# A four-stage graph network: narrow one-hots per 50 columns, and wide one-hots of two and three tiles in turn

## The reference

```
h = max(layernorm(x), 0);  x = x + L0(h)   # 4 rounds of y = segment_sum(weight * y[dst], src)
h = max(layernorm(x), 0);  x = x + L1(h)   # second stage, one round
h = max(layernorm(x), 0);  x = x + L2(h)   # two rounds by relation type, log_softmax
h = max(layernorm(x), 0);  x = x + L3(h)   # last stage, one round
```

```
# second stage: bx, by are 4 hat functions each of the edge's two attributes
msg = sum over u, v of bx[u] * by[v] * (h[dst] @ W[u, v])          # [edges, 16]
out = segment_sum(msg, src, 12500)
# last stage: 8 attributes per edge
m   = silu(einsum('ei,ej,ijh->eh', h[dst], edge_attr_8, W) / sqrt(128))
out = segment_sum(m @ W_lin / 4, src, 12500)
```

## Time and profile before

| | |
|---|---|
| time before | 18148.49 us, median of 3 (18147.04 to 18175.33) |
| profiled execution | span 18161.1 us from its first to its last instruction, 349,411 instructions; it gives no other time of its own |
| busy over the span | PE 15098.9 us (83%), DVE 14620.2 (81%), ACT 11849.6 (65%), POOL 10508.1 (58%) |
| second stage, `conv` | first `product` at 8874.0 us, last at 10899.5 us, 330 of them |
| last stage, `message` | first `product` at 15873.0 us, last at 17955.2 us, 330 of them |
| granted TensorE clock | 1.00 in both stages' loops, 0.897 on average over the span |

### The profile page before, as it was taken

The page is one execution under the profiler, slowest core; times in us unless marked ns, Lnnn a source line. Parts: engine busy times, 40 slices in busy tenths (PEclk is TensorE's granted clock), DMA queues, the critical chain, the costliest instruction groups (busy, mean ns, idle before and its releaser), DMA issues. The chain is left out here.

```text
span 18161.1 us, 349411 instructions
## 1 busy us (share of the span) xinstructions
PE 15098.9 (83%) x83251; PEld 13315.7 (73%) x83252; DVE 14620.2 (81%) x36172; ACT 11849.6 (65%) x23181; POOL 10508.1 (58%) x29948
## 2 busy tenths in 40 slices
PE   0148847998998999899699998999969999499997
PEld 0048846887887888789688885777747777399996
DVE  4745557887887888788699997999958888499997
ACT  2000026777777777678577777888858888377775
POOL 0458836775775775777477765666622424376610
PEclk9555558999999999999899999999989999699998
DMA  7611121010000100000211112222211212111111
GB/s 233 125 26 40 40 78 27 23 24 22 23 24 22 24 24 23 23 24 24 34 31 31 31 25 65 73 71 72 74 43 61 67 61 67 33 31 31 30 27 17
DMA packets 1268447, 826.81 MB, mean 46 GB/s; under 512 B 873458, under 2 KB 1213398, under 8 KB 1260758
## 3 DMA queue, kind: packets, MB, share of 16 engines
q1 hardware_dynamic: 880918, 671.78, 13.2%
q0 software_dynamic: 269056, 117.80, 3.5%
q10 hardware_dynamic: 118080, 33.61, 1.0%
HBM read 587.33 MB, written 235.06 MB: 45 GB/s over the span
## 5 line engine op out<-in xcount | busy, mean ns | idle before, releaser
L1548 PE MATMUL powers_sums<-powers_b_hot,powers_spread 128*128 128x224 f32 x26400 | 5284.7, 361 | 670.8 <-DVE powers_b_hot L1529 455.7
L1548 PEld LDWEIGHTS powers_sums<-powers_b_hot,powers_spread 128*128 128x128 f32 x26400 | 5097.4, 195 | 860.3 <-issue 826.7
L1650 POOL DMA_INDIRECT filled<-powers_by_b,powers_at_start x2688 | 3364.3, 1252 | 1721.6 <-issue 847.3
L2351 PE MATMUL relate_got<-relate_hot,relate_table 112*128 112x512 f32 (+1 forms) x10560 | 3091.5, 435 | 110.8 <-ACT relate_hot L2313 70.5
L1543 ACT ACTIVATE powers_b_hot<-powers_away,ones 128x672 f32<-128x672 f32 x2640 | 1977.9, 751 | 1251.6 <-PE powers_sums L1548 880.1
L1537 ACT ACTIVATE powers_away<-wide,powers_minus_b 128x224 f32<-128x224 f32 x6600 | 2717.6, 472 | 117.5 <-ACT powers_minus_b L1718 35.0
L2351 PEld LDWEIGHTS relate_got<-relate_hot,relate_table 112*128 112x128 f32 x10560 | 1702.7, 191 | 1388.5 <-issue 1315.0
L1526 DVE TENSOR_TENSOR powers_spread<-powers_a_hot,powers_message 128x640 f32<-128x640 f32 x2640 | 2154.4, 816 | 517.5 <-PE powers_sums L1548 327.8
L2313 ACT ACTIVATE relate_hot<-relate_away,ones 112x1280 f32<-112x1280 bf16 x1320 | 1797.9, 1362 | 734.3 <-PE relate_got L2351 447.3
L1529 DVE TENSOR_SCALAR powers_b_hot<-wide,powers_b_val 128x224 f32<-128x224 f32 x6600 | 1918.5, 339 | 0.0
L2366 PE MATMUL relate_mixed<-relate_mix,relate_picked 128*128 128x128 f32 x13200 | 1711.4, 277 | 107.3 <-issue 92.2
(11 more groups left out here) (475 smaller groups left out, 25622.2 us busy)
## 6 DMA issues: line engine op xcount, KB each, us to landing
relate_codes<-pair_rows SPq DMA_DIRECT2D x264, 800.0 KB
powers_given<-filled SPq DMA_DIRECT2D x528, 200.0 KB
rec<-relate_running SPq DMA_DIRECT2D x132, 400.0 KB
filled<-powers_by_b,powers_at_start POOLq DMA_INDIRECT x2688
grouped<-order_blanks POOLq DMA_DIRECT2D x20, 1320.0 KB
filled<-order_blanks SPq DMA_DIRECT2D x20, 1320.0 KB
held_recs<-grouped SPq DMA_DIRECT2D x132, 200.0 KB
conv_given<-filled SPq DMA_DIRECT2D x132, 200.0 KB
```

The source lines that it names most:

```text
L1548: mm = pe.matmul(gathering.sums[:, bass.ds(group * STRIDE, WINDOW)], spread[:, j].rearrange("p a d -> p (a d)"), b_hot[:, j, :], start=Fal ...
L1650: pool.indirect_dma_start(filled, bass.IndirectOffsetOnAxis(to, 0), rows, None).then_inc(spread_out[block % 2], 16)
L2351: mm = pe.matmul(got[:, n % 2, at:to], table[:, n // SLOTS % 2, half, :], flat[:, at:to], start=half == 0, stop=half == 1, skip_group_chec ...
```

## The change

`a_hot`, `b_val` and ScalarE's `minus_b` are made once for a pair (50 columns, two halves of an iteration as buffers) instead of once for a unit (10 columns). `own` becomes a pair of numbers, one for each slot of a unit: (2, 3) in the second stage, (2, 2) in the last. In the second stage the slot with 3 tiles makes them with one `tensor_tensor` compare of 3 x 224 instead of three `tensor_scalar` compares, and ScalarE makes 3 tiles of the first slot and 2 of the second.

```diff
@@ -1519,12 +1519,16 @@
     return dram.rearrange("(h p) d -> p h d", p=P)
 
 
-def spread_slot(dve, message, a_hot, spread, b_val, b_hot, c, ready, own):
+def spread_slot(dve, message, a_hot, spread, b_val, b_hot, c, ready, own, at_once=False):
 
 
     n = message.shape[1]
     dve.tensor_tensor(spread, a_hot.unsqueeze(3).to_broadcast([P, n, 8, D]),
                       message.unsqueeze(2).to_broadcast([P, n, 8, D]), ALU.mult)
+    if at_once:
+        dve.tensor_tensor(b_hot[:, 0:own, :], b_val[:, 0:own].unsqueeze(2).to_broadcast([P, own, WINDOW]),
+                          c.wide[:].unsqueeze(1).to_broadcast([P, own, WINDOW]), ALU.is_equal).then_inc(ready, 1)
+        return
     for j in range(own):
         ins = dve.tensor_scalar(b_hot[:, j, :], c.wide[:], b_val[:, j:j + 1], None, ALU.is_equal)
     ins.then_inc(ready, 1)
@@ -1780,8 +1784,8 @@
         fourth = half if hats else s.sb("fourth", [P, UNIT, 2, D])
         message = s.sb("message", [P, 2, UNIT, D])
         active = s.sb("active", [P, 2, UNIT, D]) if silu_scale is not None else message
-        a_hot = s.sb("a_hot", [P, 2, UNIT, 8])
-        b_val = s.sb("b_val", [P, 2, UNIT])
+        a_hot = s.sb("a_hot", [P, PAIRS_PER, PAIR * TURN, 8])
+        b_val = s.sb("b_val", [P, PAIRS_PER, PAIR * TURN])
         spread = s.sb("spread", [P, SPREADS, TILES, 8, D])
         b_hot = s.sb("b_hot", [P, SPREADS, TILES, WINDOW])
         if hats:
@@ -1794,9 +1798,9 @@
             turns_of, rows_of, across = 2, TILES * D, P
         mix = s.sb("mix", [rows_of, 1 if hats else TILES, P])
         turned = s.sb("turned", [rows_of, 2, turns_of, P])
-        own = 3 if hats else 2
-        away = s.sb("away", [P, 2, TILES - own, WINDOW])
-        minus_b = s.sb("minus_b", [P, 2, UNIT])
+        own = OWN if hats else (2, 2)
+        away = s.sb("away", [P, 2, TILES - min(own), WINDOW])
+        minus_b = s.sb("minus_b", [P, PAIRS_PER, PAIR * TURN])
         measured, warmed, copied_b, gate_act, gate_pe = (
             s.sem(n) for n in ("measured", "warmed", "copied_b", "gate_act", "gate_pe"))
         still, rested = s.sb("still", [P, RESTS]), s.sem("rested")
@@ -1943,20 +1947,24 @@
             def warm(it, first, j):
 
                 u = it * UNITS + j
-                act.copy(minus_b[:, j % 2], G.minus_b[:, bass.ds(u * UNIT, UNIT)]).then_inc(copied_b, 1)
-                act.wait_ge(copied_b, u + 1)
+                h, at = j // PER_PAIR, j % PER_PAIR * UNIT
+                if at == 0:
+                    pair = it * PAIRS_PER + h
+                    act.copy(minus_b[:, h], G.minus_b[:, bass.ds(pair * (PAIR * TURN), PAIR * TURN)]).then_inc(copied_b, 1)
+                    act.wait_ge(copied_b, pair + 1)
                 for part in range(2):
                     if not (first and j == 0):
                         act.sem_inc(gate_act, 1)
                         act.wait_ge(warmed, 2 * u + part - 1)
-                    away_from(act, c, minus_b[:, j % 2, part * TILES + own:(part + 1) * TILES], away[:, part], measured)
+                    away_from(act, c, minus_b[:, h, at + part * TILES + own[part]:at + (part + 1) * TILES],
+                              away[:, part, 0:TILES - own[part]], measured)
                 for part in range(2):
                     slot = 2 * j + part
                     act.wait_ge(measured, 2 * u + part + 1)
                     if not first or slot >= SPREADS:
                         act.sem_inc(gate_act, 1)
                         act.wait_ge(taken, 2 * u + part - SPREADS + 1)
-                    warm_slot(act, c, away[:, part], b_hot[:, slot % SPREADS, own:TILES], warmed)
+                    warm_slot(act, c, away[:, part, 0:TILES - own[part]], b_hot[:, slot % SPREADS, own[part]:TILES], warmed)
 
             if hats:
                 act.wait_ge(set_up, 1)
@@ -2026,17 +2034,20 @@
                                   along[:, j // PER_PAIR, at:at + UNIT].unsqueeze(2).to_broadcast([P, UNIT, 4, D]),
                                   ALU.mult).then_inc(zed, 1)
 
-            def scatter(u, j, first):
-
-                dve.wait_ge(mid, u + 1)
+            def scatter(it, j, first):
+
+                u = it * UNITS + j
+                h, at = j // PER_PAIR, j % PER_PAIR * UNIT
+                dve.wait_ge(mid, it * PAIRS_PER + h + 1)
                 dve.wait_ge(summed if silu_scale is None else activated, u + 1)
                 for part in range(2):
                     slot = 2 * j + part
                     if not first or slot >= SPREADS:
                         dve.wait_ge(taken, 2 * u + part - SPREADS + 1)
                     tiles = slice(part * TILES, (part + 1) * TILES)
-                    spread_slot(dve, active[:, j % 2, tiles], a_hot[:, j % 2, tiles], spread[:, slot % SPREADS],
-                                b_val[:, j % 2, tiles], b_hot[:, slot % SPREADS], c, ready, own)
+                    cols = slice(at + part * TILES, at + (part + 1) * TILES)
+                    spread_slot(dve, active[:, j % 2, tiles], a_hot[:, h, cols], spread[:, slot % SPREADS],
+                                b_val[:, h, cols], b_hot[:, slot % SPREADS], c, ready, own[part], at_once=own[part] == 3)
 
             scans(0, 0, 0, D)
             if hats:
@@ -2064,11 +2075,11 @@
                                       co.unsqueeze(3).to_broadcast([P, UNIT, v_wide, D]), ALU.mult).then_inc(times, 1)
                     if not first or j >= 2:
                         dve.wait_ge(ready, 2 * (u - 1))
-                    dve.tensor_tensor(a_hot[:, j % 2], G.a[:, bass.ds(u * UNIT, UNIT)].unsqueeze(2)
-                                      .to_broadcast([P, UNIT, 8]),
-                                      c.free[:, 0:8].unsqueeze(1).to_broadcast([P, UNIT, 8]), ALU.is_equal)
-                    dve.tensor_scalar(b_val[:, j % 2], G.minus_b[:, bass.ds(u * UNIT, UNIT)], -1.0, None, ALU.mult
-                                      ).then_inc(mid, 1)
+                    if jj == 0:
+                        cols = bass.ds((it * PAIRS_PER + h) * (PAIR * TURN), PAIR * TURN)
+                        dve.tensor_tensor(a_hot[:, h], G.a[:, cols].unsqueeze(2).to_broadcast([P, PAIR * TURN, 8]),
+                                          c.free[:, 0:8].unsqueeze(1).to_broadcast([P, PAIR * TURN, 8]), ALU.is_equal)
+                        dve.tensor_scalar(b_val[:, h], G.minus_b[:, cols], -1.0, None, ALU.mult).then_inc(mid, 1)
                     dve.wait_ge(times, u + 1)
                     dve.tensor_tensor(half[:], product[:, :, 0:v_wide // 2, :], product[:, :, v_wide // 2:v_wide, :],
                                       ALU.add).then_inc(added, 1)
@@ -2080,10 +2091,10 @@
                     dve.tensor_tensor(message[:, j % 2], fourth[:, :, 0, :], fourth[:, :, 1, :], ALU.add
                                       ).then_inc(summed, 1)
                     if not (first and j == 0):
-                        scatter(u - 1, (j - 1) % UNITS, first)
+                        scatter(it if j else it - 1, (j - 1) % UNITS, first)
 
             ends_loop(dve, ITS, body)
-            scatter(ALL_UNITS - 1, UNITS - 1, False)
+            scatter(ITS - 1, UNITS - 1, False)
 
         @block.tensor
         def _(pe):
```

## The result

The changed kernel takes 18338.35 us (median of 4, 18319.51 to 18358.76), the kernel before 18147.76 (median of 4): ratio 1.0102, 95% interval 1.0088 to 1.0117. It is slower by 190 us where I forecast 131 us faster; the time lies outside the range. The profiled execution has a span of 18356.6 us, 195.5 above the one of before.

What follows compares the result with a forecast made beforehand. VectorE was taken to bound the second stage, VectorE and TensorE the last. Wide one-hots 122 us, narrow operations 5 and 4, sum 131 us faster: 18017 us against the median 18148.5, range 17990 to 18070.

Steps and rivals of the forecast that it cites:

- What bounds the kernel before: VectorE bounds the second stage, busy 489.7 us of 500; the last stage belongs to both TensorE and VectorE.
- The price of the new compare: Second stage: the tensor_tensor compare of 672 takes 0.77 us, at 1.1 ns an element, bounds 0.74 and 0.79.
- The stretch: VectorE's compares lengthen while GpSimd works: runs of three by 0.09 us, runs of two by 0.015; counted as saved.
- VectorE's own sum: Second stage: 0.37 us saved per unit by the wide one-hots, 122 us in all; new unit 5.77 us.
- GpSimd, late next: Second stage: with fewer compares GpSimd's transfers fall from 1210 ns to near 1.07 us; it ends near 10700, before the loop.
- a sign of being wrong: The prediction is wrong if the second stage ends with GpSimd.
- the rival's 86 us: GpSimd keeps its pace and ends the second stage: at most 86 us gained there, time 18058 us; chance 9%.
- The lock: Claim cited from the skill: VectorE in a 2-port mode and GpSimd lock each other out; the new compare isn't stretched.
- The narrow part: Narrow operations once per pair: half starts 0.86 us after product in four units of five; 5 and 4 us gained.
- ScalarE: Second stage: ScalarE's work rises to 5.60 us per unit at worst, under the new unit of 5.77; costed at nothing.

Runs made afterwards that it cites:

- wide23: Kernel before with VectorE's wide one-hots of the second stage 2 and 3 tiles in turn, each tile by its own compare; ratio 0.9949 to the kernel before.
- last_once: Kernel before with the two wide one-hots of each last-stage slot made by one tensor_tensor compare of 448; last stage 2183.1 us, 2166.3 before.
- once22: Changed kernel with two tiles in each second-stage slot, each pair by one tensor_tensor compare of 448; second stage 2005.0 us, 2311.6 in the changed kernel.
- sep3: Changed kernel with the second stage's slot of three tiles made by three compares again, not by one; ratio 0.9976 to the kernel before.
- once_only: Kernel before with only the second stage's wide one-hots changed: 2 and 3 tiles in turn, the 3 in one compare; ratio 1.0051 to the kernel before.
- swap32: Changed kernel with second-stage slots swapped: 3 tiles by one compare first, then 2 by their own compares; second stage 2076.1 us, 2311.6 in the changed kernel.
- pair22: Changed kernel with one wait on ready per pair and 2 wide one-hots in each second-stage slot, each by its own compare; ratio 0.991 to the kernel before.
- one_wait: Changed kernel with VectorE's wait on ready only in units that make a_hot; second stage 2248.4 us, last 2162.6, against 2311.6 and 2186.6 in the changed kernel.

## Why the prediction was wrong

**What bounds the kernel before: right.** VectorE bound the second stage; `wide23` gains by taking work from it.

**The price of the new compare: right.** 0.77 forecast, 0.768 measured from start to start. The Trainium skill's tier table ("VectorE: DVE Perf Modes") had the exchange of three compares for one as a loss on VectorE; the trace gives it as even, as read.

**The stretch: right in size, wrong in meaning.** The group of VectorE's `tensor_scalar` compares, second stage, of the changed kernel (8900 to 9900 us) and then of `wide23` (9700 to 10400 us):

```profile
L1533 DVE TENSOR_SCALAR conv_b_hot<-wide,conv_b_val 128x224 f32<-128x224 f32 x330 | 95.7, 332 | 0.0
```

```profile
L1533 DVE TENSOR_SCALAR conv_b_hot<-wide,conv_b_val 128x224 f32<-128x224 f32 x592 | 179.0, 352 | 0.0
```

A run of two takes 95.7 / 165 = 0.580 us, as forecast (0.58 to 0.60). In `wide23` a run of two and one of three take 179.0 / 118.4 = 1.51 us together, where 0.59 + 0.91 was read of before. But I took the stretch as a cost of VectorE's that could be saved. It was the place where GpSimd got in. VectorE's own sum held: without its waits for GpSimd the changed unit is 5.82 us for a forecast 5.77, and the 0.05 between them is the narrow part's (below).

**"GpSimd, late next": the step that failed.** I laid 1210, 1115 and 989 ns beside 0.97, 0.63 and 0 `tensor_scalar` compares per microsecond and drew a line through them to 1.07 us, with the last transfer near 10700 us and the loop's end near 10808 to wait for. It took 1.55 us, and GpSimd ended at 11104. That count was the wrong variable. In `last_once` it is zero and transfers take 1089 ns, in `once22` zero and 1168; in the changed kernel it was under half of before and transfers took 1547. What mattered was what stands around the compare, and the one compare in place of three is what did the harm (`sep3`, `once_only` beside `wide23`). The sum was then right about VectorE (the loop ends 36 us earlier despite 74 us of waits for GpSimd, 110 in all, of a forecast 127) and void, since the stage ends with the engine that I had costed as getting faster, which the prediction itself names as a sign of being wrong. With GpSimd at its old pace the rival's 86 us would have been the gain; it had a chance of 9%, and I had bounded GpSimd's transfer only from below. By my own rule a price without a row needs both ends: a transfer's mean beside `tensor_tensor` operations had no row, and 1.5 us wasn't excluded by anything.

**The lock, half used.** In the changed kernel a transfer that starts beside the new compare waits through it and `z` and ends beside `product` (2.43 us in the timeline above; it ends 0.84 us after the record of `z`, as transfers let in at that boundary do). Before the change others waited through scans and `z`. The compare, `z` and the scans all read two operands in SBUF; `product` reads one of its two from PSUM. But `spread` and `message` read two in SBUF as well, and there transfers were let in. For the stretch I had cited the Trainium skill ("SBUF — State Buffer", "there are two physically separate sides") for the 2-port mode alone. The same section says that a VectorE operation with two SBUF inputs takes the shared pair as well, against a GpSimd operation that reads SBUF: that spoke against this change, and I left it out. The trace agrees with it in those waits. It doesn't bear it out as a rule for the pace: `swap32` has the same operations as the changed kernel in another order, and its transfers take 1.23 us, with 24 of 24 let in between the new compare and `spread`; in `last_once` compares of the new form take the place of all others, and they take 1.09.

**The narrow part: the term was mis-sized.** "A successor starts 0.04 us after its source's record ends" came from instructions with one wait. `half` would now have two, `ready` and `times`, and it started 0.10 after: 0.92 and 1.58 us for my 0.86 and 1.51. In the second stage that is 4 x 0.922 + 1.312 us per pair for 5 x 0.958, 0.21 more, 14 us over 66 pairs. So 5 and 4 us gained became 16 and 20 to 23 lost. With one wait it is 0.85 and 1.51 and the 4 us of the last stage are there. That the two narrow operations hid `product`'s latency was right.

**ScalarE: right.** 418.6 of 500 us, and it isn't the bound. With six distances a unit, in `pair22`, it is busy 482 to 486, no more than TensorE.

**What stays open.** How a transfer takes the port, and why a boundary between the same two operations lets it in in one order of the unit and not in another (16 of 38 between `spread` and the compare in the changed kernel, 123 of 123 in `swap32`). That a transfer needs the port more than once would fit; no run here shows it. Two tries that would bear on the first weren't made: the compare reading one of its inputs from PSUM, and GpSimd without its rests (`still`).

## What to carry to other kernels

Before taking instructions off the busiest engine, ask which of them let another engine in, and look at the second-latest engine's finish: here 53 us of slack stood against a stage that was to end 127 us sooner. An operation that is even on its own engine can make a neighbour's transfers a quarter longer (1210 to 1547 ns), and it shows first as longer records there; a different order of the same work took most of it back (1226). A wait that a larger buffer has made needless should go with it: a second wait ahead of a dependent instruction cost 0.07 us in each of four units of five.

## What the runs showed of the hardware

- A GpSimd indirect transfer takes 0.96 us (median) when VectorE's loop isn't running. In the changed kernel those that began beside the second `spread` took 2.43 us in the median where `z` and `product` follow the new compare, and 3.21 where scans follow; in `swap32`, with a `spread` behind the compare, 1.24.
- Three `tensor_tensor` compares of 224 shut it out as one of 672 did (1598 and 1555 ns), and two of 448 per unit did not (1168 ns).
- In the traces of before and changed, waiting transfers were let in without exception at four boundaries: `spread` to a `tensor_scalar` compare (372), `z` to `product` (368), `half` to `message` (191), and the new compare to `given` (32). Between scans, or a scan and `z`, it was 4 of 463.
- A VectorE operation that depends on the one ahead starts 0.035 us after its record ends with one wait and 0.10 with two (`one_wait` beside the changed kernel).
- The transfers of the changed kernel keep to a few places of VectorE's unit: 154 of 693 begin 3.59 to 3.68 us after `product`, so a bad place is hit again and again.
